# Sorting tokens by expert: the last mixture of a four-layer kernel on 31 padded tiles

## What is computed

```python
gu_s = x2 @ shared_w_gate_up.T
g_s, u_s = jnp.split(gu_s, 2, axis=-1)
shared_out = jax.nn.silu(g_s) * u_s @ shared_w_down.T
probs = jax.nn.softmax(x2 @ gate_w.T, axis=-1)
topk_vals, topk_idx = jax.lax.top_k(probs, 2)
topk_vals = topk_vals / jnp.sum(topk_vals, axis=-1, keepdims=True)
combine = jnp.sum(jax.nn.one_hot(topk_idx, 16) * topk_vals[..., None], axis=1)
g, u = jnp.split(jnp.einsum('th,eih->eti', x2, w_gate_up), 2, axis=-1)
out_e = jnp.einsum('eti,ehi->eth', jax.nn.silu(g) * u, w_down)
moe_out = jnp.einsum('eth,te->th', out_e, combine)
```

## Time and profile before

| | |
|---|---|
| median of 3 runs | 3320.5 us (3319.59 to 3325.22) |
| profiled execution, first to last instruction (span) | 3324.5 us; no other time of it is on record |
| TensorE, busy share of the span | 96% |
| VectorE | 65% |
| ScalarE | 51% |
| GpSimd | 26% |
| first mixture, first weight load to last down product | 2322 to 2480 us |
| last mixture, first load to end | 2943 to 3324.5 us |
| DMA | 452 MB, all but instructions on SP's queue |

### The profile page before, as it was taken

The page is one execution under the profiler, slowest core; times in us unless marked ns, Lnnn a source line. Parts: engine busy times, 40 slices in busy tenths (PEclk is TensorE's granted clock), DMA queues, the critical chain, the costliest instruction groups (busy, mean ns, idle before and its releaser), DMA issues. The chain is left out here.

```text
span 3324.5 us, 55156 instructions
## 1 busy us (share of the span) xinstructions
PE 3185.9 (96%) x18912; PEld 2815.0 (85%) x18912; DVE 2156.2 (65%) x3275; ACT 1702.5 (51%) x3206; POOL 872.7 (26%) x703
## 2 busy tenths in 40 slices
PE   8999998999999999999999999898988989889999
PEld 8898886999999998999989999786778878868887
DVE  4333334888888887888878888544555667745555
ACT  3332344666666666667666666323425445532222
POOL 0000121444444443444444444321003223400000
PEclk9999998999999999999999999999998999989999
DMA  7665785777766766776667775574201101111111
GB/s 251 217 210 193 241 269 167 160 161 163 164 159 161 160 160 152 162 159 160 159 153 161 160 161 125 161 238 164 73 31 38 30 26 36 39 39 47 46 39 44
DMA packets 360308, 452.24 MB, mean 136 GB/s; under 512 B 32316, under 2 KB 289644, under 8 KB 360072
## 3 DMA queue, kind: packets, MB, share of 16 engines
q1 hardware_dynamic: 360072, 449.22, 51.1%
HBM read 201.45 MB, written 113.43 MB: 95 GB/s over the span
## 5 line engine op out<-in xcount | busy, mean ns | idle before, releaser
L707 POOL TENSOR_TENSOR a_t_lo<-a_turned,a_t_hi 128x512 fp32r<-128x512 f32 x512 | 649.8, 1291 | 939.8 <-ACT a_t_hi L836 939.8
L827 ACT ACTIVATE a_probs<-a_ps_s,a_neg_max 128x1024 f32<-128x1024 f32 (+1 forms) x512 | 529.5, 1034 | 476.0 <-DVE a_neg_max L879 470.1
L872 DVE TENSOR_REDUCE a_half_max<-a_ps_s 128x1 f32<-128x1024 f32 (+1 forms) x512 | 571.2, 1116 | 189.5 <-PE a_ps_s L724 185.3
L722 PE MATMUL a_ps_s<-a_k_buf,a_q_buf 128*128 128x512 f32 (+1 forms) x1024 | 419.7, 410 | 18.2 <-ACT a_probs L827 11.9
L723 PE MATMUL a_ps_s<-a_k_buf,a_q_buf 128*128 128x512 f32 (+1 forms) x1024 | 386.1, 377 | 0.0
L724 PE MATMUL a_ps_s<-a_k_buf,a_q_buf 128*128 128x512 f32 (+1 forms) x1024 | 385.3, 376 | 0.0
L908 DVE TENSOR_TENSOR a_x_lo<-a_ps_x,a_x_hi 128x512 fp32r<-128x512 f32 (+1 forms) x512 | 314.5, 614 | 107.8 <-ACT a_x_hi L845 107.8
L454 DVE TENSOR_TENSOR p_out<-p_ps_j,p_out 128x512 fp32r<-128x512 f32 (+3 forms) x196 | 153.0, 781 | 326.6 <-ACT p_out L383 326.6
L898 DVE STREAM_TRANSPOSE a_turned<-xn 128x512 f32<-128x512 f32 x512 | 357.8, 699 | 1.6 <-POOL a_t_lo L707 1.6
L383 ACT ACTIVATE p_out<-p_ps_j 128x512 fp32r<-128x512 f32 (+3 forms) x196 | 141.9, 724 | 339.8 <-PE p_ps_j L288 339.7
L722 PE MATMUL a_ps_o<-a_t_hi,a_v_buf 128*128 128x256 f32 x1024 | 298.8, 292 | 6.2 <-issue 3.6
(11 more groups left out here) (319 smaller groups left out, 7389.7 us busy)
## 6 DMA issues: line engine op xcount, KB each, us to landing
xn<-a_probs SPq DMA_DIRECT2D x1024, 128.0 KB, 3.4
a_q_all<-p_out SPq DMA_DIRECT2D x64, 512.0 KB
a_q_buf<-a_q_all SPq DMA_DIRECT2D x128, 256.0 KB, 3.3
a_k_buf<-a_k_all SPq DMA_DIRECT2D x64, 464.5 KB, 4.0
a_v_all<-p_out SPq DMA_DIRECT2D x56, 512.0 KB
a_k_all<-p_out SPq DMA_DIRECT2D x48, 384.0 KB
a_v_buf<-a_v_all SPq DMA_DIRECT2D x64, 256.0 KB
a_o_all<-a_o_part SPq DMA_DIRECT2D x128, 128.0 KB, 3.0
```

Source lines behind the costliest of these rows:

```text
L707: pool.tensor_tensor(t_lo[:, slot, :, :], turned[:, slot, :, :], t_hi[:, slot, :, :].bitcast(F32), ALU.subtract).then_inc(t_done, 1)
L722: pe.matmul(o, w_hi, m_hi, start=first, stop=False)
L827: act.activation(probs[j][u.a][:, lo:hi], s_flat[:, lo:hi], ACT.Exp, bias=neg_max[:, j:j + 1], scale=SCALE, accum_out=half_sum[:, bass.ds( ...
L872: dve.reduce_max(half_max[:, half:half + 1], s_flat[:, lo:hi], AX.X).then_inc(max_done, 1)
```

## The change

The 16 routed experts are taken out of the units; the four quarters of the shared expert stay. Each token's two choices (2048 rows) get a place in an array of 3968 slots, 31 tiles of 128, in which each expert's rows begin at a tile's border, so that a tile has one expert.

- In the first mixture the 16 experts' weights, three 128x512 matrices each, are transposed by TensorE after every down product, two at a time (`turn_weight`), copied by ScalarE from `ps_t` to a half of `xn`, and stored to `wt_all` in DRAM. SP loads four ahead (`load_turn`, `store_turn`). It also writes zeros to the 3968 slots of `slots_x`.
- In the last mixture, after the first shared unit, 17 fp32 matmuls (`count_places`) count for each choice the rows before it; eight steps of VectorE (`give_places`) make slot numbers of that, and later the expert of each tile (`give_owners`). GpSimd scatters `xn` to `slots_x` by 16 indirect DMAs of 128 rows.
- After the fourth unit a loop over 31 tiles, written out: SP reads the tile's expert from SBUF into a register and loads 768 KB of weights from that address, and 256 KB of rows; TensorE transposes the rows, multiplies them with both up matrices side by side (12 matmuls of 256 columns), transposes the product, and makes the down product (three matmuls of 512 columns); VectorE copies it out and SP stores 256 KB to `slots_y`.
- At the end GpSimd gathers both rows of each token by 16 indirect DMAs, and VectorE adds them with their weights (`combine`).

The routing decides which weights a tile loads, not how many tiles there are. The diff, cut to its core (the steps of ScalarE, the split of the shared units and the allocations are left out):

```diff
+            def load_turn(n):
+                e, job = n // TURN_JOBS, n % TURN_JOBS
+                if n >= RING:
+                    sp.wait_ge(turn_ps, n - RING + 1)
+                if job < 2:
+                    sp.dma_start(turn_raw[:, n % RING, :], w_gate_up[e, job * P:(job + 1) * P, :]).then_inc(turn_loaded[n % RING], 16)
+                else:
+                    sp.dma_start(turn_raw[:, n % RING, :].rearrange("p (c i) -> p c i", c=D // P),
+                                 w_down[e].rearrange("(c p) i -> p c i", p=P)).then_inc(turn_loaded[n % RING], 16)
+
+            def store_turn(n):
+                sp.wait_ge(turned_done, n + 1)
+                sp.dma_start(wt_all[n // TURN_JOBS, n % TURN_JOBS, :, :], turned[:, n % RING, :]).then_inc(turned_stored[n % RING], 16)
+
+            load_expert(0)
+            load_expert(1)
+            sp.wait_ge(zeros_set, 1)
+            sp.dma_start(slots_x.rearrange("(j p) d -> p j d", p=P),
+                         zeros[:, :].unsqueeze(1).to_broadcast([P, slots_x.shape[0] // P, D])).then_inc(slots_zeroed, 16)
+            sp.wait_ge(xt_ps, TILES)
+            sp.wait_ge(magnitude_done, TILES)
+            for n in range(RING):
+                load_turn(n)
+            load_expert(2)
+            for n in range(TURNS):
+                store_turn(n)
+                if n + RING < TURNS:
+                    load_turn(n + RING)
+            sp.wait_ge(slots_zeroed, 16)
+            for i in range(RING):
+                sp.wait_ge(turned_stored[i], 16 * TURNS // RING)
...
                 return pe.matmul(out, w_lo, m_hi, start=False, stop=last)
+
+            def turn_weight(n):
+                pe.wait_ge(turn_loaded[n % RING], 16 * (n // RING + 1))
+                if n >= 2:
+                    pe.wait_ge(turned_done, n - 1)
+                for c in range(DC):
+                    tr = pe.transpose(ps_t[:, n % 2, c * P:(c + 1) * P], turn_raw[:, n % RING, c * P:(c + 1) * P], ident[:, :])
+                tr.then_inc(turn_ps, 1)
...
                     mm.then_inc(y_ps, 1)
+                    for i in range(PER_TILE):
+                        turn_weight(PER_TILE * n + i)
...
+                for n in range(PER_TILE * TILES * e, PER_TILE * TILES * (e + 1)):
+                    act.wait_ge(turn_ps, n + 1)
+                    if n >= RING:
+                        act.wait_ge(turned_stored[n % RING], 16 * (n // RING))
+                    act.activation(turned[:, n % RING, :], ps_t[:, n % 2, :], ACT.Copy).then_inc(turned_done, 1)
...
+            def load_owner(j):
+                a = j % RAWRING
+                if j >= RAWRING:
+                    sp.wait_ge(u_done, j - RAWRING + 1)
+                    sp.wait_ge(d_done, j - RAWRING + 1)
+                e = sp.value_load(owner_index[0:1, j:j + 1], min_val=0, max_val=E - 1)
+                sp.dma_start(w_raw[:, a, :, :], wt_all[bass.ds(e, 1), :, :, :].rearrange("o j p n -> p (o j) n")
+                             ).then_inc(tw_loaded[a], 16)
+
+            def store_slots(j):
+                sp.wait_ge(y_taken, j + 1)
+                sp.dma_start(slots_y[P * j:P * (j + 1), :], y_out[:, j % YRING, :]).then_inc(y_stored[j % YRING], 16)
...
-            load(0, 0, *routed(0))
-            load(1, 0, *routed(1))
-            with sp.Fori(1, E // 2) as i:
-                for a in range(2):
-                    load(a, JOBS * (2 * i + a - 1), *routed(2 * i + a))
-            with sp.Fori(0, SHARED // 2) as i:
-                for a in range(2):
-                    load(a, JOBS * (E + 2 * i + a - 1), *shared(2 * i + a))
+            for n in range(N):
+                load(n)
+            sp.wait_ge(owners_done, 1)
+            load_owner(0)
+            load_owner(1)
+            sp.wait_ge(scattered, 16 * GROUPS)
+            load_slots(0)
+            load_slots(1)
+            for j in range(SLOT_TILES + STORE_LAG):
+                if j + 2 < SLOT_TILES:
+                    load_owner(j + 2)
+                    load_slots(j + 2)
+                if j >= STORE_LAG:
+                    store_slots(j - STORE_LAG)
...
+            pool.wait_ge(slots_done, 1)
+            for g in range(GROUPS):
+                pool.indirect_dma_start(slots_x, bass.IndirectOffsetOnAxis(ap=slot_index[:, g:g + 1], axis=0),
+                                        xn[:, g % TILES, :], None).then_inc(scattered, 16)
+            for j in range(SLOT_TILES):
+                pool.wait_ge(d_hi_done, j + 1)
+                pool.tensor_tensor(d_lo[:, j % DOWNRING, :], w_raw[:, j % RAWRING, 2, :], d_hi[:, j % DOWNRING, :].bitcast(F32),
+                                   ALU.subtract).then_inc(d_done, 1)
+            pool.wait_ge(scattered, 16 * GROUPS)
+            pool.wait_ge(u_done, SLOT_TILES)
+            pool.wait_ge(d_done, SLOT_TILES)
+            for a in range(YRING):
+                pool.wait_ge(y_stored[a], 16 * len(range(a, SLOT_TILES, YRING)))
+            for t in range(TILES):
+                for k in range(TOP):
+                    g = TILES * k + t
+                    pool.indirect_dma_start(taken[k][:, t, :], None, slots_y,
+                                            bass.IndirectOffsetOnAxis(ap=slot_index[:, g:g + 1], axis=0)).then_inc(y_gathered[t], 16)
...
-            def expert(last, n, a, pair, following=True):
-
-                for slot in range(TC * 4):
-                    up(n, last, a, slot // 4, slot % 4)
-                    if slot >= 6:
-                        down(n, last, a, slot - 6)
-                    elif last is not None:
-                        down(last, None, 1 - a, slot + 2)
-                    if slot in (0, 2, 6) and following:
-                        transpose_weights(n + 1, 1 - a, pair, (0, 2, 6).index(slot))
...
+            def count_places():
+                pe.wait_ge(w_done, JOBS * 2)
+                pe.wait_ge(pads_set, 8)
+                pe.wait_ge(chosen_done, 1)
+                pe.matmul(t_flat(place_ps), before[:, :], t_flat(chosen[:, :, :]), start=True, stop=False)
+                for s in range(1, GROUPS + 1):
+                    mm = pe.matmul(t_flat(place_ps[:, s:GROUPS + 1, :]), ones[:, :], t_flat(chosen[:, 0:GROUPS + 1 - s, :]),
+                                   start=False, stop=s == GROUPS)
+                mm.then_inc(places_ps, 1)
...
+            def slots_up(j):
+                pe.wait_ge(s_done, j + 1)
+                pe.wait_ge(u_done, j + 1)
+                if j < 2:
+                    pe.wait_ge(gated_done, TC * N)
+                else:
+                    pe.wait_ge(s_act_done, j - 1)
+                for c in range(DC):
+                    mm = three(ps_h[:, j % 2, 0, 0:2 * I], s_hi[:, j % 2, c, :], s_lo[:, j % 2, c, :],
+                               u_hi[:, j % UPRING, c, :, :].rearrange("p k i -> p (k i)"),
+                               u_lo[:, j % UPRING, c, :, :].rearrange("p k i -> p (k i)"), c == 0, c == DC - 1)
+                mm.then_inc(u_ps, 1)
...
-            expert(None, 0, 0, 0)
-            with pe.Fori(0, N // 2 - 1) as i:
-                expert(2 * i, 2 * i + 1, 1, i + 1)
-                expert(2 * i + 1, 2 * i + 2, 0, i + 1)
-            expert(N - 2, N - 1, 1, None, following=False)
+            for n in range(N):
+                shared_unit(n)
+                if n == 0:
+                    count_places()
             for t in range(2, TILES):
-                down(N - 1, None, 1, t)
+                down(N - 1, t)
+            turn_slots(0)
+            for j in range(SLOT_TILES + 2):
+                if j + 1 < SLOT_TILES:
+                    turn_slots(j + 1)
+                if j < SLOT_TILES:
+                    slots_up(j)
+                if 1 <= j <= SLOT_TILES:
+                    slots_turn_act(j - 1)
+                if j >= 2:
+                    slots_down(j - 2)
...
-            expert(None, 0, 0)
-            with dve.Fori(0, N // 2 - 1) as i:
-                expert(2 * i, 2 * i + 1, 1)
-                expert(2 * i + 1, 2 * i + 2, 0)
-            expert(N - 2, N - 1, 1, following=False)
...
+                if n == 0:
+                    give_places()
+                if n == 1:
+                    give_owners()
+                    weights_of_choices()
...
+            owner_low(0)
+            slots_low(0)
+            for j in range(SLOT_TILES + 2):
+                if j + 1 < SLOT_TILES:
+                    owner_low(j + 1)
+                    slots_low(j + 1)
+                if j < SLOT_TILES:
+                    slots_product(j)
+                if 1 <= j <= SLOT_TILES:
+                    slots_act_low(j - 1)
+                if j >= 2:
+                    take(j - 2)
+            for t in range(TILES):
+                combine(t)
```

More of the change, by code:

```diff
@@ L1138, in _, with load_expert @@
         def _(sp):
-            for e in range(E):
+            def load_expert(e):
                 if e:
@@ new lines, in add, with route @@
```

(43 more changed lines are left out.)

370 lines of the change are left out of this document (253 added, 117 removed).

## The result

| | before | after |
|---|---|---|
| median of 4 runs | 3321.72 us | 3230.08 us (3222.79 to 3237.39) |
| profiled execution: time, span | span 3324.5 us | 3227.55 us, span 3225.8 us |
| ratio after to before, 95% interval | | 0.9722 (0.9703 to 0.9741) |

A forecast was written before the change was run, and what follows sets the result against it. TensorE was taken to bound the last block, so matmuls removed there are time saved; -284.3 - 1 + 114.7 + 2 + 3 + 6.5 + 30.8 - 2.5 + 36.6 = -94.2 us gave 3226.3 us, range 3196 to 3266.

The forecast's parts named there:

- What goes: Last mixture: 16 of 20 units removed at 17.77 us each, -284.3 us, and -1 for no wait on the router's copy.
- Finding the places: After the first shared unit: 17 fp32 matmuls at 6 us and 0.5 for VectorE's delayed product, +6.5 us.
- Scatter and gather: Indirect DMAs: 16 scatters hide beside the units, 16 gathers at 1.3 us plus waits, adds and output store, +30.8 us.
- g: GpSimd's price for an indirect DMA of 128 rows, taken as 1.3 us.
- Rival D: Indirect DMAs: GpSimd's price eats the whole gain at 5.2 us per 128 rows, slower from 5.4; chance 0.07.
- Turning the weights in the first mixture: First mixture: 48 turns 21.1 us, waits of 5 and 3, and smaller terms, +36.6 us, bounds 24 and 48.
- nearly full, 5 more: First mixture's remaining turns: a down product with two turns takes 3.6 us and nearly fills DMA, adding 5 us.
- the last store's 2.5: End of the first mixture: the last turned tile must land before the block ends, 2.5 us.
- What the tile loop costs: Tile loop: DMA paces it at 354 GB/s, 3.7 us a tile, +114.7 us for 31, plus 2 filling and 3 draining.
- Rival C: Tile loop: SP's wait for a store's tile delays the next loads, for example 5 us a tile, 3266 us; chance 0.08.
- Rival A: Tile loop: engines pace it, not DMA; 3.2 us a tile, 3210.8 us, VectorE full, DMA share under 0.9; chance 0.20.
- Rival B: Tile loop: TensorE's clock falls to half through waits, 5.4 us a tile, 3279 us; chance 0.06.

## Why the prediction was right, and where it was not

The stages missed by -7.3, +5.7, -1.7, +0.9 and -2.2 us, which leave -4.6 of the profiled spans: that the number came out so near is in part luck.

- **What goes** and **Finding the places**: -278.8 predicted, -280.5 measured. The 17 matmuls took 4.9 us where 6 was taken.
- **Scatter and gather**: g = 1.3 predicted, 1.25 to 1.31 measured; the end +28.3 predicted, +29.2 measured. With eight of the gathers gone the end was 6.6 us shorter, most of eight times g, so g is what it hangs on in the main. Rival D's point, 5.2 us, was far off. The 16 scatters end at 3033.9 us, hidden beside the units as forecast.
- **Turning the weights in the first mixture**: +36.6 predicted, +29.3 measured, inside the bounds of 24 and 48. The turns' own price (21.1) and the two waits (8 predicted, 6.7 measured) were right. The terms that failed are "nearly full, 5 more" and the last store's 2.5: after 2398 us TensorE waits for no load, at 288 to 291 GB/s and a share of 0.87 to 0.88 in the down phases, and the part behind the last add's start is no longer than before. The half rate for pieces of 512 B in the upper bound has no row, and no run measured these pieces alone. The zeros make the first wait, as forecast, but without them most of it comes back behind the third expert's weights.
- **What the tile loop costs**: +119.7 predicted, +125.4 measured, and **the mechanism was wrong**. The step that failed is "the loop goes at the slowest sum, and that is DMA at every rate shown". In this kernel it goes at no engine's sum: 392 GB/s were to be had for this very mix, so the DMA engines need no more than 3.3 us for a tile, where I took 354 GB/s and 3.7, and the step was 4.13. What I called each engine's "neighbours' tiles to work on" are three buffers, and a buffer's cycle, from the load's issue over 6 to 8 us of landing to the subtraction that frees it, is 11 to 12 us, as long as three tiles. By this account each delay in it is lost for good. Rival C had such a chain, by way of the store, and a price of 5 us; I put it aside with "Two tiles of lead speak against" without adding up the cycle. With the store out of the chain the step stayed, so the chain that no rival names, the buffer's own, is as long. C's time lies 36 us over the measured one because I took 5 us, not 4.1 and less in the last steps. A smaller slip: the slope gives 0.57 us for VectorE's copy, not 0.62, and it took 0.69.
- The loop's number came out by luck: my rate was too low by 0.4 us a tile, about half of the 0.84 that the ring costs, and the loop's last three steps are short. The 30 steps between copies took 114.7 us, the forecast's figure for 31 tiles; the 5.7 us it lacked lie outside them, in 10.0 us before the first copy and 0.7 for the last, where 5 were taken for filling and draining. Of the three rows of full DMA engines, the nearest to what this mix can have was 406 GB/s, which I had set aside as loads alone; a share of 1.02 at 308 GB/s does not say that 308 is all there is. Those 10 us moved 3.08 MB in 2621 packets, 1.2 KB each in the mean; the loop with four buffers moved 17.85 MB in 9349 from 3095 to 3140 us, 1.9 KB each. It was a row of another mix.
- **Rival A** gives 3.2 us a tile; with four buffers the loop comes to 3.29, and VectorE is 91% busy there (65.8 of 72.4 us). That is rival A's time with one more buffer, but not its sign, since the DMA share is 1.04 and not under 0.9. The Trainium skill (DMA: Bandwidth & Descriptors, Anatomy of one DMA) has 436 GB/s for the bytes of a DMA; 392 to 397 were measured with four buffers.
- **Rival B** came in part: 0.94 for the mean grant and 0.50 in stretches of 4 to 6 us behind a wait. In the longest step it goes with 2.3 us of slower work (5.0 for 2.7) beside 3.3 us of waiting; filling the idle time raised the grant and gave no time back. The Trainium skill (TensorE: Matmul & The Clock Gate, Part 1) says that waits for DMA in every step bring the slow clock back; the trace agrees in part, in some steps and not in all.

## What to carry to other kernels

For a loop over loaded tiles, add up a buffer's whole cycle (issue, landing under load, every step until it is free, the next issue) and divide by the number of buffers before asking whether bytes or engines pace it; here a fourth buffer with late stores was worth about 25 us of the run, 20 of them beyond late stores alone, and an earlier release in the kernel with the turns in the loop 14. A DMA share near 1 does not yet say that no more can be had (0.97 at 325 GB/s here, 1.04 at 392): look for a rate that does not rise when loads are issued earlier. Experiments that cut bytes or one chain agree with both theories where another chain of the same length stands behind; adding a buffer tells them apart.

## What was not expected

- The rate at one share: 0.97 went with 325 GB/s and 1.04 with 392, for the same transfers. Why the share is so high at the lower rate was not settled.
- GpSimd's subtraction of the down weights. In the changed kernel and in the one that turns the weights in the loop and frees its buffers early, view of the tile, ns min/median/max:

```profile
L2155 POOL TENSOR_TENSOR d_d_lo<-d_w_raw,d_d_hi x31: 1291/1812/2268, 3065.3 to 3187.3; 128x512 fp32r<-128x512 f32 x31
```

```profile
L2153 POOL TENSOR_TENSOR d_d_lo<-d_w_raw,d_d_hi x31: 1269/1289/1295, 3046.4 to 3157.0; 128x512 fp32r<-128x512 f32 x31
```

The same instruction takes 1.81 or 1.29 us. What differs is that VectorE's large subtraction beside it reads both of its inputs from SBUF in the first kernel and one of them from PSUM in the second. The Trainium skill (GPSIMD Engine Reference, Specifications) names contention with VectorE instructions of two SBUF inputs; these rows fit, though no run changed that alone.
- More transposes on TensorE made the kernel faster, since they moved out of a stage in which TensorE was full: eight a tile in the loop, 248 in all, in place of the 128 of 32 turns before it.
